# Routed token rows turned by a block exchange and VectorE instead of TensorE, with gathers eight tiles ahead and two raw weight buffers

## The chip, the cores and the metric

The kernel runs on one core of one Trainium2 chip. The metric is the device time of one execution in microseconds (us): the median of three runs. Times inside an execution come from the hardware profiler and count from the start of its span.

## The reference

The kernel computes one gated block: a state-space mixer whose result is added to x, and then a mixture of experts on the normalised sum. The part that the change touches is the second one.

```python
x = x + tanh(g_xattn) * mamba(ctx, layernorm(x))          # 4 x 512 tokens, width 512
h = layernorm(x).reshape(-1, 512)                         # 2048 tokens
scores = softmax(h @ gate_w.T)                            # 16 experts
topk_w, topk_ids = top_k(scores, 6); topk_w /= topk_w.sum(-1)
out = sum over experts e: combine[:, e] * swiglu(h, w13[e], w2[e])   # 6 of 16 per token
out = out + swiglu(h, sw13, sw2)                          # shared expert
x = x + tanh(g_ffn) * out
# swiglu(x, w13, w2): g, u = split(x @ w13.T); (silu(g) * u) @ w2.T, inner width 352 (704 shared)
```

## The kernel before

**Two stages.** For some 490 us the kernel runs the mixer, batch by batch (four batches, 16 states n, four channel blocks j per n). Orders of the side work per engine are written out by hand in tables (`PE_FIRST`, `SP_SECOND` and so on). In this stage GpSimd multiplies each scan by a row `crow` (L949), which SP loads three steps of n ahead (`c_row`, L576 to 582). When a batch's normalised rows are ready, SP stores them to a DRAM table `token_rows` (`rows`, L607), one DMA per batch, and later their 18 expert weights beside them (`weights`, L619).

**The experts** run in tiles of 128 tokens. The shared expert is cut into two of inner width 352, so there are 32 shared tiles (numbers 0 to 31, NS = 32), and then the routed tiles, each with tokens of one expert, 104 in this execution. A shared tile loads x already turned (channels on partitions) from a second table. A routed tile gathers 128 token rows by number with an indirect DMA on GpSimd (`gather`, L989) into one of four slots of `xt`, five tiles ahead (`AHEAD`), and TensorE turns it: four 128x128 transposes through an identity into PSUM bank 4 (`turn_x`, L1683). Each value is split into a high part rounded for TensorE and a low remainder, and each product is formed as high·high + high·low + low·high.

**One tile on TensorE** (`tile`, L1728), with the tile before it interleaved:

```python
up(t, s, (0, 1), off)                     # 12 products, N = 352
turn_a(t - 1, 1 - s)                      # 3 transposes, needs `am` of t-1
up(t, s, (2, 3), off)                     # 12 products
turn_x(t + 1, (s4 + 1) % 4, m)            # 4 transposes (routed tiles only)
down(t - 1, 1 - s, old)                   # 9 products, N = 512, needs `al` of t-1
```

Ahead of each routed tile TensorE's stream reads two registers from the table `meta` (`weights_of`, L1723: how many experts' weights must be there, L1724, and where they lie, L1726). Engines execute their streams in order.

**The other engines, per tile.** ScalarE: `ah` (high part of a, L862), `xh` (high part of x of the next tile, L852), silu (L857), copy of y (L868), then a register read that tells whether a new expert starts; if so it casts half of the next expert's weights (L822). VectorE: `al` (L1399), the tile's routing weight `cc` (L1372), the token numbers for the gather (`gather_ids`, L1378), `xl` (low part of x, L1363), the numbers for the output (L1383), the product `am` (L1393), and at an expert's start the other half of the cast (L1417). The copies L1372, L1378 and L1383 each follow a register read. GpSimd: gather, at an expert's start the low part of the weights (9.6 us, L987), and the accumulating indirect write of y to the output (`add`, L1011). The token numbers per expert are lists which GpSimd scatters to DRAM with 96 small DMAs beside the shared tiles and then reads back (L1060, `ids_in`).

**Weights.** One raw buffer `wraw`; SP fetches the next expert (2176 KB) as soon as the low part of the one before is done (`fetch`, L630), ScalarE's queue those of experts 1 and 2.

## Time and profile before

| | us |
|---|---|
| median of 3 runs | 1436.62 |
| lowest and highest run | 1435.21, 1438.37 |
| span of the profiled execution, core 0 | 1435.5 |
| mean granted TensorE clock | 0.976 |
| busy in the span: TensorE products / weight loads | 1349.9 / 1210.6 |
| busy: VectorE / ScalarE / GpSimd | 787.5 / 730.9 / 949.3 |

The profile gives the profiled execution's span and no other time of it; the runs' times are those of whole executions. A chain of waits, followed back from the last instruction, lies on TensorE for 65% of the span. "issue" in a row is time in which an engine waited for nothing that the profile shows. Products are pipelined: one begins while the one before still runs, so the rows' durations overlap, and the distance from start to start is what each costs. Some product records can be missing. Weight loads (PEld) and TensorE's products (PE) are shown as two engines, register reads of an engine's stream with a q behind the engine's name.

### The profile page before, as it was taken

To read this page: it belongs to the slowest core of one execution; us is meant where nothing else is said; L and a number is where in the kernel's file an instruction comes from. 1 tells how busy PE (TensorE), PEld (TensorE's weight loads), DVE (VectorE), ACT (ScalarE), POOL (GpSimd) and SP (SyncE) were. 2 spreads that over 40 slices of the span, in tenths; PEclk is the share of its full clock that TensorE was granted. 3 is DMA by queue.
4 is the path that set the end of the run, shared out by engine and by line. 5 is a ranking of instruction groups with operands and counts; after the bars stand their busy time and mean duration, and the time that the engine had idled before them with its cause. 6 is when DMAs were issued, how large, how long until landed. Compare 5 with 4: busy or idle time off the path is not lost.

```text
span 1435.5 us, 32257 instructions
## 1 busy us (share of the span) xinstructions
PE 1349.9 (94%) x8480; PEld 1210.6 (84%) x8481; DVE 787.5 (55%) x1364; ACT 730.9 (51%) x1317; POOL 949.3 (66%) x671
## 2 busy tenths in 40 slices
PE   6897998997898899999999999999999999999996
PEld 2686887887888799999998989989889988899885
DVE  6878898898989854653333333333333333333331
ACT  5898897898889464343332333323333333332321
POOL 0588898898988747887456665566645666546632
PEclk8899999999999999999999999999999999999999
DMA  4120122222242365645455435555445544454432
GB/s 137 38 74 31 53 67 96 67 73 91 75 146 72 133 129 106 142 84 141 83 141 145 131 63 144 139 147 137 104 94 137 141 135 104 95 147 131 76 68 36
DMA packets 65042, 149.13 MB, mean 104 GB/s; under 512 B 16976, under 2 KB 17616, under 8 KB 62656
## 3 DMA queue, kind: packets, MB, share of 16 engines
q0 software_dynamic: 31024, 62.10, 22.9%
q1 hardware_dynamic: 33392, 81.21, 17.5%
q10 hardware_dynamic: 560, 4.98, 1.0%
q8 instruction: 36, 0.59, 0.2%
q14 instruction: 30, 0.25, 0.1%
HBM read 101.50 MB, written 48.99 MB: 105 GB/s over the span
## 4 chain that ended last, share of the span: by engine, by line
PE 65%; DVE 3%; issue 1%; POOL 0%; ACT 0%; DVEq 0%; POOLq 0%; ACTq 0%
PE bank L1719 19%; PE bank L1699 19%; PE bank L1700 18%; PE bank L1687 3%; PE bank L1710 3%; DVE hs L1172 1%; PE bank L1604 1%; PE bank L1590 1%; PE bank L1602 0%; POOL hc L949 0%; DVE sc L1226 0%; PE bank L1665 0%; DVEq L1375 0%; DVE xl L1363 0%; DVE du L1186 0%
## 5 line engine op out<-in xcount | busy, mean ns | idle before, releaser
L949 POOL TENSOR_TENSOR hc<-hs,crow 128x512 f32<-128x512 f32 x254 | 322.6, 1302 | 91.8 <-DVE hs L1172 84.6
L1699 PE MATMUL bank<-w,xh 128*128 (+1 forms) x1088 | 368.7, 340 | 7.6 <-issue 4.2
L1015 POOL DMA_INDIRECT out_x<-ys,aid x104 | 171.2, 1646 | 275.0 <-issue 215.7
L1700 PE MATMUL bank<-w,xh 128*128 (+1 forms) x1088 | 351.2, 323 | 0.0
L1172 DVE TENSOR_TENSOR_SCAN hs<-dA,bank 128x512 f32<-128x512 f32 x256 | 295.8, 1208 | 47.9 <-PE bank L1604 32.0
L1719 PE MATMUL bank<-w,ah 128*128 (+1 forms) x816 | 264.7, 405 | 2.7 <-DVE al L1399 2.7
L1399 DVE TENSOR_TENSOR al<-bank,ah 128x384 fp32r<-128x384 f32 x136 | 75.8, 557 | 331.0 <-ACT ah L862 283.2
L1699 PEld LDWEIGHTS bank<-w,xh 128*128 128x128 f32 x1088 | 204.3, 188 | 35.9 <-issue 32.1
L1700 PEld LDWEIGHTS bank<-w,xh 128*128 128x128 f32 x1088 | 206.4, 190 | 2.3
L868 ACT COPY ys<-bank 128x512 f32<-128x512 f32 x136 | 79.9, 587 | 195.9 <-PE bank L1719 191.5
L1700 PE MATMUL bank<-w,xl 128*128 (+1 forms) x544 | 175.9, 323 | 0.0
L1699 PE MATMUL bank<-w,xl 128*128 (+1 forms) x544 | 175.7, 323 | 0.0
L1719 PEld LDWEIGHTS bank<-w,ah 128*128 128x128 f32 x816 | 145.0, 189 | 27.7 <-issue 2.2
L1590 PE MATMUL bank<-ident,hc 128*128 128x128 f32 x1024 | 160.4, 281 | 7.6 <-POOL hc L949 5.1
L862 ACT CAST ah<-bank 128x384 fp32r<-128x384 f32 x136 | 65.3, 480 | 196.9 <-PE bank L1710 166.7
L786 ACT ACTIVATE dA<-delta,aneg 128x512 f32<-128x512 f32 x256 | 164.0, 710 | 0.0
L1604 PE MATMUL bank<-bdiag,duT 128*128 128x128 f32 x1024 | 163.7, 285 | 0.0
L1719 PE MATMUL bank<-w,al 128*128 (+1 forms) x408 | 161.2, 395 | 0.0
L852 ACT CAST xh<-bank 128x512 fp32r<-128x512 f32 x104 | 61.2, 588 | 182.9 <-PE bank L1687 175.4
L987 POOL TENSOR_TENSOR w<-wraw,w 128x4352 f32 x15 | 143.8, 9588 | 0.7 <-issue 0.5
L1604 PEld LDWEIGHTS bank<-bdiag,duT 128*128 128x128 f32 x1024 | 142.5, 201 | 0.0
L1590 PEld LDWEIGHTS bank<-ident,hc 128*128 128x128 f32 x1024 | 124.3, 145 | 11.0 <-POOL hc L949 6.7
(184 smaller groups left out, 2051.7 us busy)
## 6 DMA issues: line engine op xcount, KB each, us to landing
wraw<-in_wall SPq DMA_DIRECT2D x16, 2176.0 KB
crow<-c_rows SPq DMA_DIRECT2D x64, 256.0 KB, 3.3
xt<-token_rows_turned SPq DMA_DIRECT2D x32, 256.0 KB
out_x<-ys POOLq DMA_DIRECT2D x32, 256.0 KB
wraw<-in_wall ACTq DMA_DIRECT2D x2, 2176.0 KB
token_rows<-rowb SPq DMA_DIRECT2D x4, 1028.0 KB
xrow<-in_x SPq DMA_DIRECT2D x4, 1024.0 KB, 7.0
out_x<-xrow SPq DMA_DIRECT2D x4, 1024.0 KB, 4.9
```

Of the source, the lines that this page charges most:

```text
L786: nc.scalar.activation(dA[:, 4 * (n % 2) + j, :], delta[b % 2][:, j, :], ACT.Exp, scale=aneg[:, j, n:n + 1]).then_inc(dA_done, 1)
L868: nc.scalar.copy(ys[:, slot, :], banks[7][:]).then_inc(ys_done, 1)
L949: nc.gpsimd.tensor_tensor(hc[:, j, :], hs[:, j, :], crow[:, n % 4, :], ALU.mult).then_inc(hc_done, 1)
L987: nc.gpsimd.tensor_tensor(columns(w, at + WCOLS, WCOLS), wraw[:], columns(w, at, WCOLS), ALU.subtract).then_inc(wl_done, 1)
L1015: pool.indirect_dma_start(out_rows, bass.IndirectOffsetOnAxis(ap=aid[:, s:s + 1], axis=0), ys[:, s, :], None, bounds_check=TOKENS - 1, oob ...
L1172: nc.vector.tensor_tensor_scan(hs[:, j, :], dA[:, 4 * (n % 2) + j, :], dbu[j % 2][:], 0.0, ALU.mult, ALU.add).then_inc(scanned, 1)
L1399: nc.vector.tensor_tensor(al[:, s, :], banks[5][:, 0:IP], ah[:, s, :], ALU.subtract).then_inc(al_done, 1)
L1590: mm = nc.tensor.matmul(ysum[t][:, cols], hc[:, j, t * P:(t + 1) * P], ident[:], start=n == 0 and j == 0, stop=n == DS - 1, is_transpose=T ...
L1604: mm = nc.tensor.matmul(dbu[j % 2][:, t * P:(t + 1) * P], duT[b % 2][:, t, j * P:(j + 1) * P], bdiag[:, n % 2, t - COPIED, :], start=True, ...
L1699: nc.tensor.matmul(gate_bank[:, 0:I], xx, columns(w, off + ww + k * 2 * I, I), start=first, stop=last)
L1700: mm = nc.tensor.matmul(up_bank[:, 0:I], xx, columns(w, off + ww + k * 2 * I + I, I), start=first, stop=last)
L1719: mm = nc.tensor.matmul(banks[7][:], aa, columns(w, off + ww + W2AT + k * H, H), start=k == 0 and n == 0, stop=k == IK - 1 and n == 2)
```

## The change

TensorE no longer turns x of routed tiles. Rows are stored to `token_rows` with their 512 values regrouped by 32-wide quadrants: 16 DMAs per batch and one for two more columns, in place of one. The gather goes into a new buffer `rowg`, eight tiles ahead in place of five. For each pair of tiles SP exchanges blocks between quadrants of partitions with 16 DMAs of 32 partitions x 2 tiles x 512 B from `rowg` to `xq` (which lies in `wraw`, free after the shared experts). VectorE then transposes 32x32 blocks of `xq` into PSUM bank 4 (`turn`), ahead of `al`. The routing weight is taken three tiles ahead, the token numbers seven; the first of these move to earlier shared tiles, and with them VectorE's wait for the lists. Weights of experts from 2 on are fetched on ScalarE's queue into two raw buffers `wnext`; ScalarE reads one more register per tile for it.

```diff
-AHEAD = 5
-FIRST_ROWS = {NS - 3: (NS, NS + 1), NS - 2: (NS + 2,), NS - 1: (NS + 3, NS + 4)}
+AHEAD = 8
+TAKEN = 3
+FIRST_IDS = {NS - 4: (NS, NS + 1, NS + 2, NS + 3), NS - 2: (NS + 4, NS + 5), NS - 1: (NS + 6,)}
+FIRST_TAKEN = {NS - 1: (NS, NS + 1, NS + 2)}
+FIRST_ROWS = {NS - 5: (NS, NS + 1), NS - 4: (NS + 2, NS + 3), NS - 2: (NS + 4, NS + 5), NS - 1: (NS + 6, NS + 7)}
...
+        xq = wraw[:, 0:4 * H].rearrange("p (s c) -> p s c", s=4)
...
+        rowg = alloc(ctx, "rowg", [P, 4, ROW])
+        wnext = alloc(ctx, "wnext", [P, 2 * WCOLS])
...
             def rows(b, _):
                 sp.wait_ge(norm_done, TC * (b + 1))
-                sp.dma_start(rows_v[b, :, :, 0:H + 2], rowb[:]).then_inc(rows_stored, 16)
+                    for t in range(TC):
+                        for c in range(QUAD):
+                            sp.dma_start(rows_v[b, :, t, c * P:(c + 1) * P].rearrange("p (k i) -> p k i", k=HK),
+                                         rowb[:, t, 0:H].rearrange("p (k c i) -> p c k i", k=HK, c=QUAD)[:, c]).then_inc(rows_stored, 16)
+                    sp.dma_start(rows_v[b, :, :, H:H + 2], rowb[:, :, H:H + 2]).then_inc(rows_stored, 16)
...
-            with sp.Fori(3, NX) as e:
-                fetch(e)
+            def exchange(i, h):
+                for k in (2 * h, 2 * h + 1):
+                    apart(sp, gathered[k], 16 * i + 16, "sp")
+                apart(sp, xt_turned, 4 * i + NS + 2 * h - 2, "sp")
+                for q in range(QUAD):
+                    for c in range(QUAD):
+                        sp.dma_start(xq[32 * c:32 * c + 32, 2 * h:2 * h + 2, q * P:(q + 1) * P],
+                                     rowg[32 * q:32 * q + 32, 2 * h:2 * h + 2, c * P:(c + 1) * P]).then_inc(swapped[h], 16)
...
+            with sp.Fori(0, groups) as i:
+                for h in range(2):
+                    exchange(i, h)
...
             def next_weights(t):
...
                     split_high(e, t)
+                last = act.value_load(meta[0:1, 5, bass.ds(t, 1)], min_val=0, max_val=NX - 2)
+                with act.If(last > 0):
+                    apart(act, wl_done, last, "act")
+                    fetch(last + 1)
...
-            def gather(t, s):
-                if isinstance(t, int) and t < NS + 4:
-                    pool.wait_ge(xl_done, t - 3)
-                else:
-                    apart(pool, xt_turned, t - 3, "pool")
+            def gather(t, s, m):
+                if not (isinstance(m, int) and m == 0):
+                    apart(pool, swapped[s // 2], 16 * QUAD * QUAD * m, "pool")
                     apart(pool, cc_done, t - 3, "pool")
                 apart(pool, gid_done, t + 1, "pool")
-                pool.indirect_dma_start(xt[:, s, :], None, rows_d[:, :],
+                pool.indirect_dma_start(rowg[:, s, :], None, rows_d[:, :],
...
+            def turn(t, s4, m):
+                if isinstance(t, int) and t < NS:
+                    return
+                apart(dve, swapped[s4 // 2], 16 * QUAD * QUAD * (m + 1), "dve")
+                dve.wait_ge(xh_done, t)
+                dve.wait_ge(xl_done, t)
+                nc.vector.transpose(banks[4][:].rearrange("p (k q j) -> p q k j", k=HK, q=QUAD),
+                                    xq[:, s4, :].rearrange("p (q k i) -> p q k i", q=QUAD, k=HK)).then_inc(xt_turned, 1)
...
-            def gather_ids(t, s4):
+            def gather_ids(t, s4, m):
+                if not (isinstance(m, int) and m == 0):
+                    apart(dve, gathered[s4], 16 * m, "dve")
...
-            def tile(t, s4, gathers=False, adds=False, m=None):
+            def tile(t, s4, m=0, gathers=False, takes=False, adds=False):
                 s = s4 % 2
+                turn(t + 1, (s4 + 1) % 4, m + (s4 + 1) // 4)
                 a_low(t - 1, 1 - s)
-                take_weight(t + 1, (s4 + 1) % 4, m)
...
+                    for late in FIRST_IDS.get(t, ()):
+                        gather_ids(late, late % 4, (late - NS) // 4)
+                    for late in FIRST_TAKEN.get(t, ()):
+                        take_weight(late, late % 4, (late - NS) // 4)
+                if takes:
+                    take_weight(t + TAKEN, (s4 + TAKEN) % 4, m + (s4 + TAKEN) // 4)
+                if gathers:
+                    gather_ids(t + AHEAD - 1, (s4 + AHEAD - 1) % 4, m + (s4 + AHEAD - 1) // 4)
                 x_low(t + 1, 1 - s)
...
-                if t == NS - 3:
+                if t == min(FIRST_IDS):
                     dve.wait_ge(ids_in, 16)
...
-                if more and not (isinstance(t, int) and t + 1 < NS):
-                    turn_x(t + 1, (s4 + 1) % 4, m)
                 down(t - 1, 1 - s, old() if callable(old) else old)
```

## Rows read from the trace of the kernel before

**Rows 1.** The page: busy time of an engine, and one of its costliest groups

```profile
PE 1349.9 (94%) x8480; PEld 1210.6 (84%) x8481; DVE 787.5 (55%) x1364; ACT 730.9 (51%) x1317; POOL 949.3 (66%) x671
...
L949 POOL TENSOR_TENSOR hc<-hs,crow 128x512 f32<-128x512 f32 x254 | 322.6, 1302 | 91.8 <-DVE hs L1172 84.6
```

**Rows 2.** Busy time by stretch (stretch, length, engines, granted clock, DMA share, GB/s)

```profile
1000.00:1200.00 200.00, 197.80 (x1154) 179.75 (x1153) 71.59 (x179) 66.45 (x120) 113.20 (x62) 1.00 0.48 118
```

**Rows 3.** Timeline (start, us, engine, line): `a` transposes of shared and routed tiles

```profile
675.36 0.49 PE L1710 MATMUL bank<-ident,am 128*128 128x128 f32 x3
681.65 0.49 PE L1710 MATMUL bank<-ident,am 128*128 128x128 f32 x3
694.68 0.49 PE L1710 MATMUL bank<-ident,am 128*128 128x128 f32 x3
...
1407.53 0.49 PE L1710 MATMUL bank<-ident,am 128*128 128x128 f32 x3
```

**Rows 4.** Timeline of TensorE in one routed tile; in brackets the idle time before

```profile
1005.50 0.49 PE L1710 MATMUL bank<-ident,am 128*128 128x128 f32 x3
...
1007.76 0.60 PE L1687 MATMUL bank<-ident,xt 128*128 128x128 f32 x4
1008.12 0.71 PE L1719 MATMUL bank<-w,ah 128*128 x2
...
1010.06 0.40 PE L1719 MATMUL bank<-w,al 128*128 x1
...
1010.48 0.19 PEld L1699 LDWEIGHTS bank<-w,xh 128*128 128x128 f32 x1 [0.45 <-issue]
```

**Rows 5.** Timeline of ScalarE and VectorE in the same tile

```profile
1006.02 0.48 ACT L862 CAST ah<-bank 128x384 fp32r<-128x384 f32 x1 [1.46 <-PE bank L1710]
...
1006.54 0.56 DVE L1399 TENSOR_TENSOR al<-bank,ah 128x384 fp32r<-128x384 f32 x1 [2.24 <-ACT ah L862]
...
1009.02 0.69 DVE L1363 TENSOR_TENSOR xl<-bank,xh 128x512 fp32r<-128x512 f32 x1 [0.35 <-ACT xh L852]
```

**Rows 6.** Line L1724, ns min/median/max, first and last start: that tile; 780 to 1435

```profile
L1724 PEldq TENSOR_LOAD <-meta x1: 897/897/897, 1008.0 to 1008.0; - x1
...
L1724 PEldq TENSOR_LOAD <-meta x92: 296/452/1000, 780.2 to 1411.3; - x92
```

**Rows 7.** Timeline of GpSimd, the accumulating write before that load

```profile
1005.61 1.59 POOL L1015 DMA_INDIRECT out_x<-ys,aid  x1 [4.11 <-issue]
```

**Rows 8.** Timeline of a tile in which an expert starts

```profile
845.99 2.02 ACT L822 CAST w<-wraw 128x2176 f32 x1 [0.50 <-issue]
...
850.91 0.69 DVE L1363 TENSOR_TENSOR xl<-bank,xh 128x512 fp32r<-128x512 f32 x1
...
851.86 0.43 PE L1699 MATMUL bank<-w,xh 128*128 x1 [0.24 <-DVE xl L1363]
```

**Rows 9.** The lists' load and its landing (us), and VectorE around it

```profile
678.11 0.59 POOL L1060 DMA_DIRECT2D lists<-token_lists  x1 [0.47 <-DMA token_lists<-ids,posi]
...
DMA to landing us min/median/max: 3.8/3.8/3.8
...
676.40 0.56 DVE L1399 TENSOR_TENSOR al<-bank,ah 128x384 fp32r<-128x384 f32 x1 [3.79 <-issue]
...
682.69 0.56 DVE L1399 TENSOR_TENSOR al<-bank,ah 128x384 fp32r<-128x384 f32 x1 [3.79 <-ACT ah L862]
683.83 0.15 DVE L1378 COPY gid<-lists 128x1 int32 x1 [0.58 <-issue]
```

**Rows 10.** Line L582, SP's `crow` loads: ns of an issue, and landing (us)

```profile
L582 SPq DMA_DIRECT2D crow<-c_rows x64: 319/320/1097, 23.3 to 468.1; - x64
...
DMA to landing us min/median/max: 3.0/3.3/7.8
```

**Rows 11.** Busy time by stretch around an idle spell (columns as in rows 2)

```profile
228.00:230.00 2.00, 0.37 (x4) 0.13 (x2) 1.97 (x4) 2.00 (x4) 1.57 (x3) 1.00 0.56 130
...
232.00:234.00 2.00, 2.00 (x12) 2.00 (x12) 1.28 (x2) 0.00 (x0) 1.74 (x3) 0.53 0.00 0
```

More of the change, by code:

```diff
@@ L447, in mamba_moe @@
         gathered = [sem(f"gathered{i}") for i in range(4)]
+        swapped = [sem(f"swapped{i}") for i in range(2)]
+        cc_done = sem("cc_done")
         zero_done = sem("zero_done")
@@ L608, in rows @@
                 sp.wait_ge(norm_done, TC * (b + 1))
-                sp.dma_start(rows_v[b, :, :, 0:H + 2], rowb[:]).then_inc(rows_stored, 16)
+                with nc.allow_non_contiguous_dma(reason="a row's columns by quadrant of the transposed row"):
+                    for t in range(TC):
[3 more added lines that the diff above has]
+                    sp.dma_start(rows_v[b, :, :, H:H + 2], rowb[:, :, H:H + 2]).then_inc(rows_stored, 16)
             def turned_(b, _):
@@ L886, in high_piece @@
                     act.wait_ge(down_done, TT * (e - 1))
-                nc.scalar.copy(w[:, base + at:base + at + size], wraw[:, at:at + size]).then_inc(*split(e, k, EARLY))
+                raw, first = raw_of(e)
+                nc.scalar.copy(w[:, base + at:base + at + size], raw[:, first + at:first + at + size]).then_inc(*split(e, k, EARLY))
             def last_choice(_):
@@ L1071, in _ @@
             for k in range(8):
-                if k + AHEAD < 8:
-                    gather(rest + k + AHEAD, (k + AHEAD) % 4)
                 next_weights(rest + k)
@@ L1485, in _ @@
                     dve.sem_inc(aid_done, NS)
-                tile(t, t % 4)
+                tile(t, t % 4, -1 if t < NS else 0)
                 beside(DVE_AFTER_MUL, t)
@@ L1489, in _ @@
             groups = routed_groups(dve)
-            tile(PEELED, PEELED % 4)
+            tile(PEELED, PEELED % 4, -1)
             next_weights(PEELED)
-            for k in range(1, 4):
-                tile(PEELED + k, (PEELED + k) % 4, True, True)
-                next_weights(PEELED + k)
-            with dve.Fori(0, groups - 1) as i:
+            for t in range(NS, NS + 3):
+                tile(t, t % 4, 0, gathers=True, takes=True, adds=True)
+                next_weights(t)
+            most = groups_but_2(dve)
+            with dve.Fori(0, most) as i:
                 for k in range(4):
                     t = 4 * i + NS + 3 + k
-                    tile(t, (3 + k) % 4, True, True, i + 1)
+                    tile(t, (3 + k) % 4, i + (3 + k) // 4, gathers=True, takes=True, adds=True)
                     next_weights(t)
-            last = tiles_but_12(dve) + 11
-            a_low(last - 1, 0)
-            add_ids(last, 3)
-            multiply(last, 1)
-            a_low(last, 1)
+            rest = tiles_but_12(dve) + 7
+            for k in range(4):
+                tile(rest + k, (3 + k) % 4, most + (3 + k) // 4, takes=k < 2, adds=True)
+                next_weights(rest + k)
+            a_low(rest + 3, 0)
+            add_ids(rest + 4, 3)
+            multiply(rest + 4, 3, most + 1)
+            a_low(rest + 4, 1)
         @block.tensor
@@ L1681, in beside @@
                         last_count(i)
-            def turn_x(t, s, m=None):
-                rows_in(pe, t, s, m, "pe")
-                at_least(pe, xl_done, t)
-                for k in range(HK):
-                    mm = nc.tensor.transpose(banks[4][:, k * P:(k + 1) * P], xt[:, s, k * P:(k + 1) * P], ident[:])
-                mm.then_inc(xt_turned, 1)
             def up(t, s, chunks, off):
@@ L1726, in weights_of, with tile @@
                 return pe.value_load(meta[0:1, 1, bass.ds(t, 1)], min_val=0, max_val=2 * WCOLS)
-            def tile(t, s4, old, off, more=True, m=None):
+            def tile(t, s4, old, off):
                 s = s4 % 2
@@ L1764, in _ @@
                     off = weights_of(4 * i + PEELED + k)
-                    tile(4 * i + PEELED + k, (3 + k) % 4, old, off, True, i)
+                    tile(4 * i + PEELED + k, (3 + k) % 4, old, off)
                     old = off
@@ L1770, in of_last @@
                 return pe.value_load(meta[0:1, 1, bass.ds(last - k, 1)], min_val=0, max_val=2 * WCOLS)
-            tile(last, 3, lambda: of_last(1), weights_of(last), False)
+            tile(last, 3, lambda: of_last(1), weights_of(last))
             turn_a(last, 1)
```

83 lines of the change are left out of this document (49 added, 34 removed).

## Prediction

> **What bounds the kernel now.** I read the page first, then the stretches, then single tiles. The page shows TensorE busy for 94% of the span [rows 1], the windows 98.9% of it (197.80 of 200 us) in the routed stage [rows 2]. That looks like an engine limited by its products, from which every removed microsecond comes off the end. The single tiles say something else. A shared tile, which turns no x, takes 681.65 − 675.36 = 6.29 us from one set of three `a` transposes to the next; from 694.68 to 1407.53 there are 103 periods of 6.92 us [rows 3]. The four x transposes hold the array for 1008.12 − 1007.76 = 0.36 us, and I take 0.35 [rows 4]. They explain a bit over half of the 0.63 us between the two kinds of tile.
>
> The rest is TensorE's instruction stream. In the tile whose `a` transposes start at 1005.50 (T), ScalarE rounds `a` from T+0.52, VectorE has the low half (`al`) at 1006.54 + 0.56 = T+1.60 [rows 5], and only then does the stream pass its wait, hand out `down`, and start two register loads for the next tile (`weights_of`, L1724 and L1726). The first begins at 1008.0 and takes 897 ns [rows 6]; the next tile's first weight load comes at 1010.48 = T+4.98, after 0.45 us of idling that nothing else explains ("issue") [rows 4]. The array could have begun at T+4.80: the last `down` product starts at 1010.06, and the nine are some 0.24 us apart. So there are **two limits on the start of the next tile**: the array, T+4.80, and the stream, which is 0.9 us (hand-out) + the first load + 1.58 us (1010.48 − 1008.90) behind `al`: T+4.38 with the shortest load (296 ns), T+4.98 with this one. The median load in the routed stage is 452 ns, the longest 1000 [rows 6]. The stream's limit starts at `al`, which comes before the x transposes, so removing them doesn't move it.
>
> Why loads are long: GpSimd's accumulating write of the tile before started at 1005.61, the load ended at 1008.90, 3.3 us later [rows 6, 7]. A load that begins while that write is under way ends about there.
>
> **The change part by part, against the profiled execution** (span 1435.5 us; the median of the runs shown is 1436.6, and I set the sum against that, as 1.1 us lies outside the span or is scatter).
>
> *x transposes off TensorE.* Array limit T+4.45 in place of T+4.80. Were it the only limit: 104 × 0.35 = 36 us. The stream gives part of it back. The accumulating write waits for the tile's y, and y for the end of `down`, so with `down` 0.35 us earlier the write comes earlier too. Let u be the start of a tile's successor after T: a late u puts the next T later, the write relatively earlier, its load shorter, and the next u earlier by as much. Two successive u thus add up to a constant, now about 4.80 + 4.98, afterwards 0.35 less. Each tile gains half: 0.175 us, and 104 × 0.175 = **−18.2 us**. At an expert's start the chain is another but the same holds: ScalarE's cast of weights (845.99, 2.02 us) holds back `al`, then `xl` (850.91) and the next tile to 851.86 [rows 8]; that cast follows the y of the tile before, which moves with `down`.
>
> *VectorE's turn.* The trace has no such operation. Nearest row: `xl`, 128x512 out of PSUM, 0.69 us [rows 5]; I bound it by that and twice that, 1.38, and take 0.7. It stands ahead of `al`, where VectorE sits 2.24 us until ScalarE is done [rows 5], so it costs nothing; without that cover it would be 104 × 0.7. At an expert's start the idle is shorter, and 1.38 us would cost 0.3 in 15 tiles. The Trainium skill (VectorE: DVE Perf Modes, Rules for kernel authors) says to transpose 128×128 on TensorE when PSUM will do, and gives 311 ns on VectorE for 128 columns of bf16: an estimate of 4 × 311 = 1.24 us for 512 columns, by which the sum stays as it is.
>
> *Other VectorE work.* `gather_ids` gains a wait in front of `xl`. `xl` itself needs no TensorE turn any more, but in part of the tiles it is the id copy ahead of it that decides. Two register steps, some 0.1 us: +2.4 us (0 to 5).
>
> *The start of the routed stage.* The wait for the token lists moves one tile ahead. The lists are issued at 678.11 and land 3.8 us later, at 681.9; the id copies of today come at 683.83 and just don't wait. One tile earlier VectorE stands at the `al` of 676.40 [rows 9], so it stops for 5.5 us, and TensorE with it. `down` then starts at 682.6 instead of 677.6. Four id copies follow in front of `xl`: the first 1.14 us after `al` starts (683.83 − 682.69), three more of some 0.73 (0.58 idle + 0.15), then 0.15 and `xl`, 0.69, and 0.26 to the first product (851.86 behind 850.91 + 0.69 [rows 8]): 686.4 instead of 675.36 + 4.45 = 679.8. **+6.6 us.** GpSimd sends the lists behind its own scatters of token numbers, so nothing in this change brings them sooner. In tile 31 one id and three weights stand ahead of `xl` (5.47 against 4.80): +0.7. After an idle stretch as long as this the clock may fall: at 228 to 230 the engine worked 0.37 of 2 us, and at 232 to 234 it was granted 0.53, the lower level of 1.2 GHz [rows 11]. Three microseconds at half speed lose 1.5, partly inside the wait: +1.0 (0 to 3).
>
> *The exchange.* 16 DMAs of 32 KB for two tiles on SP. An issue on SP takes 0.32 us at the median [rows 10]: 5.1 us per pair, landing some 3.3 later, against 2 × 6.7 us. With gathers eight tiles ahead a pair has about 1.5 tiles to spare. It costs nothing on the path. But it reads SBUF all through the stage, as the accumulating write does that stretches the loads: per load between nothing and the 0.6 us of 897 against 296; it can't shorten them. Pieces of 32 KB, spread out, are a thinner stream than one write of 256 KB, so I stay near the lower end: 0.02 each, **+2 us** (0 to 28; the upper end is 0.2 us, worked out under the rivals).
>
> *Weights.* The fetches move from SP to ScalarE's queue, one issue per expert behind the cast, and each tile reads one register more: about 0.6 us, within the 1.46 us that ScalarE idles before `ah` [rows 5]. On SP they would have stood ahead of the exchange. GpSimd's gather waits for later ids, still long before its write is due: nothing.
>
> *Rows stored in 16 + 1 pieces.* 17 SP issues in place of one, 5.4 us, with `crow` loads behind them. These are asked for three steps of n ahead, each four products of 1.30 us on GpSimd [rows 1]: 15.6 us, and land in 3.3, 7.8 at worst [rows 10]. 5.4 + 7.8 < 15.6: nothing (0 to 3).
>
> Sum: −18.2 + 2.4 + 6.6 + 0.7 + 1.0 + 2.0 = −5.5, so **1431.1 us**, and I say 1431. The forecast's own range is 1422 to 1440.
>
> **The rivals.**
> *The array is the only limit* (0.17). For it: 98.9% busy [rows 2]. Then −36.4 + 8.3 (list wait, tile 31, clock) = 1408. Against it: the 0.45 us "issue" ahead of the weight load [rows 4].
> *Slower, by longer register loads* (0.25). If the exchange's reads stretch the first load of each tile by 0.2 us, the stream's limit takes the gain: with every tile 0.2 later and the array no longer deciding, the steady tiles lose about 104 × 0.18 = 19 us in place of gaining 16, and the start loses 8.3: 1464. At 0.1 us gain and loss are even in the tiles and the start's loss remains: 1445. The point from which it decides is 0.05 us per load. For it: loads of 897 against 296 beside another SBUF-reading DMA; against it: gathers and weight fetches go on beside loads now, and the shortest still take 296.
> *The exchange doesn't keep pace* (0.04). Two `crow` issues took up to 1.10 us [rows 10]; 16 × 1.10 = 17.6 us per pair would bind the stage: 52 × (17.6 − 13.5) = +213, 1650. Here the Trainium skill (DMA: Bandwidth & Descriptors, Rules for kernel authors) warns that many small transfers should be coalesced and that under 64 KB it is mostly overhead. By that rule this rival would get more; the row's median of 0.32 speaks against it.
> *Nothing to see* (0.09): the steady gain comes to about 9 us and the start's loss eats it, 1436.
>
> **How the numbers follow.** About 0.2% (2.9 us) is what a measurement of this kernel can tell from no change. The forecast holds 0.45; by its own range about 0.07 of it lies within 0.2% and 0.02 above. Faster: 0.17 + 0.36 = 0.53. Same: 0.07 + 0.09 = 0.16. Slower: 0.25 + 0.04 + 0.02 = 0.31. For 8 in 10 the range reaches from the array's case, 1408, to 1450, which leaves out the worse half of the slower case and the lost pace.
>
> **What would show it.** Right: tile periods near 6.75 in the routed stage with weight loads idle on "issue"; a gap of about 5 us on TensorE at 677 to 683; `al` still 1.6 us behind the `a` transposes. Wrong: periods of 6.4 (the array alone), first loads above 0.5 us at the median (the stretch), TensorE or VectorE waiting for `xq` (the pace), or no gap at the start.

## The result and the profile after

The changed kernel takes 1491.52 us (median of 4 runs, 1488.31 to 1493.88) beside 1437.49 us for the kernel before on the same chip: a ratio of 1.0374 with an interval of 1.0354 to 1.0394. It is 54 us slower, where 6 us less were forecast. The profiled span went from 1435.5 to 1492.0 us, the mean granted clock from 0.976 to 0.955.

TensorE has 11 us less work (1338.9 against 1349.9 us [rows 1]) and is idle longer. These are the page's line of busy times and the windows row that answers to [rows 2]:

```profile
PE 1338.9 (90%) x8064; PEld 1184.5 (79%) x8065; DVE 857.2 (57%) x1469; ACT 732.2 (49%) x1317; POOL 949.1 (64%) x671
...
1000.00:1200.00 200.00, 181.36 (x966) 161.25 (x965) 83.37 (x189) 62.30 (x111) 107.59 (x56) 0.96 0.62 148
```

In the same 200 us TensorE worked 181.36 us, before 197.80. Where it stood idle is told by its waits in the routed stage (700 to 1440; columns: us in total, times, longest):

```profile
PE bank L1772 <- DVE am L1452: 42.2, 10, 5.3
PE bank L1761 <- issue: 14.2, 42, 1.0
PE bank L1761 <- DVE xl L1410: 4.2, 7, 1.1
PE bank L1781 <- DVE al L1458: 3.5, 10, 0.8
```

The first line is new: ten waits ahead of the `a` transposes (`turn_a`, now L1772) for VectorE's `am`, up to 5.3 us each. I write T for the start of a tile's three `a` transposes, as in the prediction. Here is the timeline around one such wait. Tile 58, in which an expert starts, has T = 914.91:

```profile
914.91 0.49 PE L1772 MATMUL bank<-ident,am 128*128 128x128 f32 x3
...
929.69 0.99 POOL L1041 DMA_INDIRECT rowg<-token_rows,gid  x1 [9.46 <-issue]
930.85 9.59 POOL L1033 TENSOR_TENSOR w<-wnext,w  x1 [0.18 <-issue]
...
934.88 0.49 PE L1772 MATMUL bank<-ident,am 128*128 128x128 f32 x3
940.61 1.59 POOL L1059 DMA_INDIRECT out_x<-ys,aid  x1 [0.17 <-issue]
...
946.25 0.15 DVE L1441 COPY aid<-lists 128x1 int32 x1 [7.62 <-DMA out_x<-ys,aid]
946.51 0.58 DVE L1452 SCALAR_TENSOR_TENSOR am<-sg,cc,bank 128x352 f32<-128x352 f32 x1
...
947.15 0.90 PE L1772 MATMUL bank<-ident,am 128*128 128x128 f32 x3 [5.32 <-DVE am L1452]
```

Read it upwards. TensorE waits for `am`, `am` stands behind the id copy `aid` on VectorE, `aid` waits 7.62 us for the landing of the accumulating write of four tiles earlier (four slots), and that write was issued at 940.61, T+25.7. Its y had been copied by 920.46 (T+5.6); it stood behind the 9.6 us low part of the weights (`split_low`), and that behind the gather, which GpSimd issued only at T+14.8 after 9.46 us of waiting. In the kernel before, the same three instructions at an expert's start are these, with the start of that tile, 52, and the `aid` of four tiles later:

```profile
846.66 0.49 PE L1710 MATMUL bank<-ident,am 128*128 128x128 f32 x3
...
848.91 0.98 POOL L997 DMA_INDIRECT xt<-token_rows,gid  x1 [0.30 <-issue]
849.91 9.58 POOL L987 TENSOR_TENSOR w<-wraw,w 128x4352 f32 x1
859.65 1.58 POOL L1015 DMA_INDIRECT out_x<-ys,aid  x1 [0.16 <-issue]
...
871.95 0.15 DVE L1383 COPY aid<-lists 128x1 int32 x1 [0.36 <-issue]
```

Gather at T+2.2, write at T+13.0, `aid` at T+25.3. No `aid` waited for a write there; after the change ten do (who waited for the write's line L1059 from 700 to 1430, and its landing):

```profile
  DVE aid L1441: 64.0, 10
...
DMA to landing us min/median/max: 4.6/5.4/11.5
```

What did the gather wait for? It writes a slot of `rowg` that the exchange of four tiles earlier reads. This is the exchange's line, first for the 16 DMAs of that pair, then for the whole run (ns of an issue, min/median/max), with who waited for it in the whole run:

```profile
L688 SPq DMA_DIRECT2D wraw<-rowg x16: 594/602/1103, 910.8 to 921.0; - x16
...
  POOL rowg L1041: 9.5, 1
...
L688 SPq DMA_DIRECT2D wraw<-rowg x832: 588/597/1517, 692.8 to 1446.4; - x167
...
  POOL rowg L1041: 178.9, 25
  DVE bank L1426: 12.6, 9
```

An issue takes 0.60 us, so a pair takes 11.3 us here (910.8 to 922.1), and after the last issue the gather still waits until 929.69, while the next expert's weights pass: ScalarE asked for them at 915.07, and the DMA engines are full from 915 to 925 (windows, the last but one column is their share):

```profile
915.00:920.00 5.00, 4.71 (x26) 3.79 (x24) 2.57 (x7) 2.50 (x5) 3.94 (x3) 1.00 0.95 323
920.00:925.00 5.00, 5.00 (x31) 4.85 (x32) 2.07 (x5) 1.89 (x4) 0.23 (x1) 1.00 1.02 303
```

The pairs that the gathers of the nine stalled starts wait for land 6.5 to 9.1 us after their last issue has ended, the other 43 pairs 1.3 us after it at the median and 4.7 at the most.

All fifteen expert starts fit. Two tiles share one exchange, so only the gather in an even tile, the first of its pair, meets this wait. In the nine starts in even tiles (32, 38, 52, 58, 64, 70, 84, 90, 116) the gather goes at T+13.8 to T+15.3 and the write at T+24.6 to T+26.1, and the third and fourth period after the start (T of tile t+3 to T of tile t+5 for a start in tile t) are together 3.6 to 7.1 us longer than the same two before: 53.6 us. In the six in odd tiles (45, 77, 97, 103, 109, 123) the write goes at T+16.1 to T+20.8, and these two periods differ by −0.4 to +0.9 us. Part of each stall is the clock after it: in all nine the granted clock fell to 0.50, for 3.4 to 6.9 us. In tile 61 TensorE works 0.83 of 6 us, and then runs at half speed, the level of 1.2 GHz, for 3 us (windows; the granted clock is the third column from the right):

```profile
941.00:947.00 6.00, 0.83 (x6) 0.53 (x4) 0.65 (x2) 0.00 (x0) 4.78 (x5) 0.76 0.66 111
947.00:950.00 3.00, 2.85 (x11) 2.86 (x12) 1.41 (x4) 1.06 (x2) 2.56 (x2) 0.50 0.89 175
```

The second loss is at the start. VectorE's `al` stops as forecast, but longer:

```profile
674.04 0.35 ACTq L880 DMA_DIRECT2D wnext<-in_wall  x1
...
682.84 0.59 POOL L1104 DMA_DIRECT2D lists<-token_lists  x1 [4.85 <-DMA token_lists<-ids,posi]
685.57 0.56 DVE L1458 TENSOR_TENSOR al<-bank,ah 128x384 fp32r<-128x384 f32 x1 [12.61 <-DMA lists<-token_lists]
...
688.92 0.71 DVE L1410 TENSOR_TENSOR xl<-xt,xh 128x512 fp32r<-128x512 f32 x1
```

The lists are issued at 682.84 instead of 678.11 [rows 9], since GpSimd waits 4.85 us for its scatters to land, before 0.5.

**The account**, from T to T: tiles 26 to 30 are 10.6 us longer, 30 to 32 0.6, the nine stalls 53.6, the other 84 tiles up to 134 are 9.8 us shorter, the shared tiles before 0.2 longer: 55.2 of the 56.5 us by which the spans differ; the rest lies before the first and after the last tile.

### The profile page after: what moved, and what is told of

Same layout as the page of the kernel before. It is cut to its first block, busy times and chain, and to the rows that moved or that the text cites. A ratio compares the mean times of both kernels' runs of the same rounds, so it can differ in the third digit from the quotient of the medians.

```text
span 1492.0 us, 33495 instructions
## 1 busy us (share of the span) xinstructions
PE 1338.9 (90%) x8064; PEld 1184.5 (79%) x8065; DVE 857.2 (57%) x1469; ACT 732.2 (49%) x1317; POOL 949.1 (64%) x671
## 3 DMA queue, kind: packets, MB, share of 16 engines
q0 software_dynamic: 31024, 62.10, 22.6%
## 4 chain that ended last, share of the span: by engine, by line
PE 27%; DMA 10%; SPq 9%; issue 9%; POOL 7%; DVE 4%; POOLq 2%; DVEq 2%; ACTq 1%; ACT 1%
SPq L688 9%; PE bank L1781 8%; PE bank L1761 7%; PE bank L1762 7%; POOL token_lists L1071 5%; DMA rowg<-token_rows,gid 5%; DMA wraw<-rowg 2%; DMA out_x<-ys,aid 2%; PE bank L1772 2%; POOL out_x L1053 1%; DVE hs L1214 1%; DVEq L1430 1%; POOLq L1076 1%; POOLq L1082 1%; PE bank L1673 1%
## 5 line engine op out<-in xcount | busy, mean ns | idle before, releaser
L1761 PE MATMUL bank<-w,xh 128*128 (+1 forms) x1088 | 379.1, 349 | 20.4 <-issue 15.3
L1762 PE MATMUL bank<-w,xh 128*128 (+1 forms) x1088 | 357.0, 329 | 0.0
L1781 PE MATMUL bank<-w,ah 128*128 (+1 forms) x816 | 261.0, 401 | 15.1 <-DVE al L1458 15.0
L1041 POOL DMA_INDIRECT rowg<-token_rows,gid x104 | 105.0, 1010 | 265.3 <-issue 195.1
L1761 PEld LDWEIGHTS bank<-w,xh 128*128 128x128 f32 x1088 | 209.6, 193 | 60.6 <-issue 57.7
L1059 POOL DMA_INDIRECT out_x<-ys,aid x104 | 168.3, 1618 | 102.4 <-ACT ys L908 45.1
L1762 PEld LDWEIGHTS bank<-w,xh 128*128 128x128 f32 x1088 | 211.3, 194 | 1.4
L1781 PEld LDWEIGHTS bank<-w,ah 128*128 128x128 f32 x816 | 152.3, 192 | 43.5 <-issue 10.3
L1762 PE MATMUL bank<-w,xl 128*128 (+1 forms) x544 | 178.5, 328 | 0.0
L1761 PE MATMUL bank<-w,xl 128*128 (+1 forms) x544 | 178.4, 328 | 0.0
L1033 POOL TENSOR_TENSOR w<-wnext,w x15 | 144.0, 9600 | 0.8 <-issue 0.2
```

The source lines that it names most:

```text
L1033: nc.gpsimd.tensor_tensor(columns(w, at + WCOLS, WCOLS), columns(raw, source, WCOLS), columns(w, at, WCOLS), ALU.subtract).then_inc(wl_don ...
L1041: pool.indirect_dma_start(rowg[:, s, :], None, rows_d[:, :], bass.IndirectOffsetOnAxis(ap=gid[:, s:s + 1], axis=0)).then_inc(gathered[s], 16)
L1059: pool.indirect_dma_start(out_rows, bass.IndirectOffsetOnAxis(ap=aid[:, s:s + 1], axis=0), ys[:, s, :], None, bounds_check=TOKENS - 1, oob ...
L1761: nc.tensor.matmul(gate_bank[:, 0:I], xx, columns(w, off + ww + k * 2 * I, I), start=first, stop=last)
L1762: mm = nc.tensor.matmul(up_bank[:, 0:I], xx, columns(w, off + ww + k * 2 * I + I, I), start=first, stop=last)
L1781: mm = nc.tensor.matmul(banks[7][:], aa, columns(w, off + ww + W2AT + k * H, H), start=k == 0 and n == 0, stop=k == IK - 1 and n == 2)
```

## The experiments

The table holds the two stretches of each profiled execution, T26 to T32 (start) and T32 to T134 (102 routed periods); executions differ by up to 4.6 us before tile 26 (T26 lies between 664.96 and 669.55), which these leave out. Ratios are against the kernel before, on the same chip; e2, e3 and e4 are single runs, and only their times stand. e2 and e5 leave a part of the routed x out of the computation.

| run | time, us | ratio (interval) | T26 to T32 | T32 to T134 |
|---|---|---|---|---|
| before | 1437.5 | 1 | 39.1 | 707.0 |
| after | 1491.5 | 1.0374 (1.0354 to 1.0394) | 50.4 | 750.9 |
| e1 gather last | 1441.1 | 1.0026 (1.0011 to 1.0042) | 49.5 | 702.0 |
| e2 half the exchange | 1439.2 | | 50.1 | 697.7 |
| e3 fetch two tiles later | 1449.0 | | 49.9 | 706.1 |
| e4 third fetch in tile 22 | 1485.8 | | 46.3 | 748.3 |
| e5 before, one x transpose | 1423.5 | 0.9909 (0.9889 to 0.9930) | 38.7 | 693.2 |
| e6 e1 + start | 1439.6 | 1.0017 (1.0005 to 1.0029) | 46.4 | 699.1 |
| e7 e6, write held | 1441.3 | 1.0030 (1.0016 to 1.0045) | 47.1 | 700.9 |
| e8 before, write held | 1478.9 | 1.0302 (1.0281 to 1.0323) | 39.1 | 748.4 |
| e9 before, loads ahead of `down` | 1443.3 | 1.0028 (1.0013 to 1.0044) | 39.7 | 712.3 |
| e10 e6, loads ahead of `down` | 1432.9 | 0.9965 (0.9952 to 0.9978) | 46.3 | 693.5 |
| e11 e10, scatters earlier | 1433.4 | 0.9963 (0.9950 to 0.9976) | 46.7 | 695.9 |
| e12 before, loads ahead of `turn_a` | 1487.6 | 1.0339 (1.0321 to 1.0357) | 41.8 | 752.7 |
| e13 after, all edits, loads as e12 | 1477.4 | 1.0278 (1.0260 to 1.0296) | 43.4 | 740.7 |
| e14 before, loads ahead in two of four | 1431.9 | 0.9961 (0.9946 to 0.9975) | 39.3 | 701.0 |
| e15 after, all edits, loads as e14 | 1426.6 | 0.9911 (0.9892 to 0.9930) | 40.9 | 692.0 |

**What makes the write late (e1, e2, e3).** Three things stand one behind the other: the exchange's 16 issues, the weight fetch beside its landing, and the order on GpSimd. Each run takes away one.

```diff
 e1, GpSimd's routed loop
-                    gather(t + AHEAD, (k + AHEAD) % 4, i + (k + AHEAD) // 4)
                     next_weights(t)
                     expert_starts(t, k)
                     add(t, k)
+                    gather(t + AHEAD, (k + AHEAD) % 4, i + (k + AHEAD) // 4)
 e2, exchange (and its two counts halved)
-                    for c in range(QUAD):
+                    for c in range(0, QUAD, 2):
 e3, ScalarE's next_weights
-                last = act.value_load(meta[0:1, 5, bass.ds(t, 1)], ...
+                last = act.value_load(meta[0:1, 5, bass.ds(t - 2, 1)], ...
```

> The changed kernel with one edit: in GpSimd's routed loop the gather stands behind the accumulating write of the tile in place of ahead of everything. Theory A (GpSimd's order): at an expert's start in an even tile the gather waits for an exchange until 13.8 to 15.3 us after the tile's a transposes (T), the 9.6 us split_low and the tile's write are queued behind it (write at T+25), and VectorE waits four tiles later for that write. With the gather last, split_low starts at about T+4 and the write at about T+14, as in the kernel before; the nine stalls of 3.6 to 7.1 us (53.6 us in sum) go: 1491.5 - 53.6 = 1438, between 1430 and 1448, and no wait of VectorE's id copy (aid) on the write is left above 1 us. Rival B (the exchange's own pace: 16 issues of 0.60 us for two tiles, landing up to 6.9 us late): the gathers now go no earlier than before, at expert starts later, so the exchange comes later still and VectorE's turn waits for it: 1480 to 1510.

> The changed kernel with 8 in place of 16 exchange DMAs for two tiles: half of the 32x32-block columns of each routed x are not moved (left out of the computation). Theory A, as to where the time is lost: the exchange of a pair ends 8 x 0.62 = 5 us earlier, an even expert start's gather goes at about T+9 to T+10, its write at about T+20, where the six starts in odd tiles have it today without a stall: the nine stalls go or fall under 1 us each, 1438 to 1446. Rival C (the weight fetch on ScalarE's queue is what makes the exchange late, by 5.6 to 6.9 us between last issue and landing): the shorter exchange overlaps the fetch as much and lands as late: stalls shrink by less than half, 1465 to 1485.

> The changed kernel with ScalarE asking for the weights of the expert after next two tiles after an expert's start in place of at the start. Rival C (the fetch beside the exchange makes it land late): the exchange that an even expert start's gather waits for lands about 5 us earlier, the write goes at about T+20, and the nine stalls go: 1438 to 1446; the odd starts may get stalls of their own if the fetch now meets their exchange. Theory A with the issue cost alone deciding: the gather's time moves by less than 2 us and the stalls stay at 4 to 6 us each: 1475 to 1490.

e1 came out at 1441, within Theory A's range. At the start in tile 58 (T = 894.50) GpSimd now does this:

```profile
894.50 0.49 PE L1772 MATMUL bank<-ident,am 128*128 128x128 f32 x3
896.98 1.00 POOL L1041 DMA_INDIRECT rowg<-token_rows,gid  x1 [0.30 <-issue]
898.00 9.62 POOL L1033 TENSOR_TENSOR w<-wnext,w  x1
...
907.78 1.58 POOL L1059 DMA_INDIRECT out_x<-ys,aid  x1 [0.17 <-issue]
```

The gather there is the tile before's; `split_low` starts at T+3.5 and the write at T+13.3, as in the kernel before. No wait of `aid` for a write is left, nor any of `turn_a` for `am`; the nine stalls come to 0.9 us in place of 53.6, and T32 to T134 falls by 48.8 us. The exchange keeps up: VectorE's turn waits for it 12.1 us in seven tiles. Rival B falls.

e2 (1439) and e3 (1449) take away nearly as much, 53.1 and 44.8 us, with GpSimd's order left as it was. So no single part is the cause. In the changed kernel the writes at the fifteen starts land 4.5 to 5.1 us after their issue, and one that went by about T+20 held TensorE up by 0.6 us at the most (in e3, with writes at T+16.0 to T+22.6, by 1.7); to pass that it took the long exchange, the fetch beside it and the 9.6 us behind the wait together. Rival C's expectation for e2 fell and Theory A's for e3 fell, by the same fault: each took one part to be enough by itself. What the three runs share is the place, the wait in front of `split_low` and the write.

**The same stall in the kernel before (e8).** Here the exchange and its issues don't exist; the write alone is held back, by 5.5 us at the median of the tiles in and just behind which no expert starts (T+12.3 in place of T+6.8). Meant as a test of the register loads (below), it shows the stall.

```diff
                     expert_starts(t, k)
+                    apart(pool, xl_done, t + 4, "pool")
                     add(t, k)
```

> The kernel before, its x transposes kept, with the same hold of GpSimd's accumulating write behind VectorE's xl. Theory L: tiles whose first register load is short take 6.74 us there, those with the write at the a transposes 7.00 (66 of 102); all at 6.74 is (6.93 - 6.74) x 102 = 19 us less, 1418, between 1414 and 1424, with the median first load 0.30 in place of 0.41 us. Rival (the array alone is the limit, loads don't matter): 1434 to 1440.

It came out 3% slower. These are the start in tile 58 (T = 893.17) with the landing of its write, TensorE's waits from 700 to 1440, and who waited for the write from 700 to 1430:

```profile
901.14 0.98 POOL L997 DMA_INDIRECT xt<-token_rows,gid  x1 [0.31 <-issue]
902.15 9.59 POOL L987 TENSOR_TENSOR w<-wraw,w 128x4352 f32 x1
...
911.90 0.33 SPq L633 DMA_DIRECT2D wraw<-in_wall  x1
911.91 1.59 POOL L1015 DMA_INDIRECT out_x<-ys,aid  x1 [0.17 <-issue]
...
DMA to landing us min/median/max: 10.4/10.4/10.4
...
PE bank L1711 <- DVE am L1394: 35.0, 13, 4.4
...
  DVE aid L1384: 60.4, 13
```

The held write of the tile before pushes the gather to T+8.0 and `split_low` to T+9.0; the write comes at T+18.7 in place of T+13, and thirteen tiles wait for `am`. A kernel without any exchange stalls in the same place once GpSimd is some 6 us late at an expert's start. I had priced that lateness at nothing. What counts is when the write has landed: in this kernel SP fetches the next weights in the moment in which the write goes (911.90), and the writes at fourteen of the fifteen starts land 9.2 to 10.4 us after their issue, so that T+18.7 is too late here and would not be in the changed kernel.

The third and fourth periods after the fifteen starts are together 44.5 us longer than in the kernel before. The rest of the 102 periods gain 3.2 us, although the first register load of a tile now takes 0.303 us at the median (700 to 1400) in place of 0.385. The 19 us that Theory L gave to short loads did not come.

**The start (e4, e6, e11).**

```diff
 e4
-               8: [("exp", 3)], TT - 3: [("fetch", 2)], NS - 5: [("fetch", 3)]}
+               8: [("exp", 3)], TT - 3: [("fetch", 2)], NS - 10: [("fetch", 3)]}
 e6: e1, e4 and
-FIRST_IDS = {NS - 4: ...
+FIRST_IDS = {NS - 3: ...
-FIRST_ROWS = {NS - 5: (NS, NS + 1), NS - 4: (NS + 2, NS + 3), ...
+FIRST_ROWS = {NS - 4: (NS, NS + 1), NS - 3: (NS + 2, NS + 3), ...
 e11: e10 and
-LISTS_LATE = 2
+LISTS_LATE = 1
```

> The changed kernel with the fetch of the third expert's weights (2.2 MB, ScalarE's queue) in tile 22 in place of tile 27. Theory S (the start's extra loss): this fetch, at 674.0, runs beside the last scatters of token numbers, which land 4.3 us later than before (GpSimd waits 4.85 in place of 0.5 us for them), so the lists go out at 682.8 in place of 678.1 and the first routed tiles come that much later. With the fetch done before, GpSimd waits under 1 us, the lists go out at about 678, the gap between the a transposes of tiles 26 and 27 is 12.3 in place of 17.0 us and the whole 4.7 us less: 1487. Rival: the scatters land late for another reason (rows stored in pieces, the small descriptors): nothing changes, 1491.

> The changed kernel with three edits: the gather last in GpSimd's routed loop (as alone in e1), the fetch of the third expert's weights in tile 22 (as alone in e4), and the first token ids and gathers one tile later, where the kernel before waits for the lists. If the terms add: 1441 (e1) - 4.7 (lists sooner) - 1 (part of the wait for the lists hidden again; the chain lists, gather, 16 exchange issues, turn is some 19 us long and binds the first routed tile in either place): 1435, between 1431 and 1439, level with the kernel before.

> e10 with GpSimd's scatters of token numbers one tile earlier throughout (they begin one tile after the shared stage's first tile in place of two, and end 3 to 6 us earlier), so that the lists land before VectorE asks for them and the chain lists, gather, exchange, turn begins sooner: 4 to 6 us less than e10. Rival (the first exchange is bound by SP's issues whatever the lists do, or GpSimd's writes are late now): no change against e10.

e4's lists and the `al` that waits for them:

```profile
675.87 0.59 POOL L1104 DMA_DIRECT2D lists<-token_lists  x1 [0.45 <-DMA token_lists<-ids,posi]
679.75 0.56 DVE L1458 TENSOR_TENSOR al<-bank,ah 128x384 fp32r<-128x384 f32 x1 [9.33 <-DMA lists<-token_lists]
```

GpSimd waits 0.45 us again; tiles 26 to 30 take 32.1 us in place of 36.3, against 25.6 before. So with the lists on time the wait that the change moved ahead costs 6.5 us, against the 6.6 for the wait and 1.0 for the clock of the prediction, and the fetch beside the scatters the other 4.2. e6, with 1439.6 just above its range, gains nothing at the start by asking later: 46.4 as in e4, the loss only passes to tiles 30 to 32, where the turn waits up to 9.1 us for the first exchange. e11 sends the lists a tile sooner and gains nothing either, with the tile in which they are asked for as late as in e10. Lists sooner and asked for in the changed kernel's tile (e13, e15) do it: 43.4 and 40.9 us.

**What the x transposes are worth (e5).**

```diff
-                for k in range(HK):
+                for k in range(1):
                     mm = nc.tensor.transpose(banks[4][:, k * P:(k + 1) * P], xt[:, s, k * P:(k + 1) * P], ident[:])
```

> The kernel before with one in place of four x transposes per routed tile: three quarters of the routed x are left out of the computation (xl and xh are taken from a bank of which three quarters are not written anew). It measures the term x transposes off TensorE by itself, 3/4 of it. The prediction's half share (two limits, array and instruction stream, in turn): 104 x 0.75 x 0.35 / 2 = 13.7 us less: 1423, between 1419 and 1427. Rival (the array is the only limit): 104 x 0.75 x 0.35 = 27.3 us less: 1409, between 1405 and 1413. Rival (the instruction stream alone decides): within 3 us of 1437.

1423.5 us, and T32 to T134 13.9 us shorter where the half share said 13.7. The half share holds; scaled to four transposes it is 18.5 us, the prediction 18.2. What halves the gain, e5 doesn't show by itself.

**The stream's register loads (e7, e9, e10, e12 to e15).** Once the stalls are gone the routed tiles take 6.85 to 6.88 us (e6, e1), and by my estimate the array would allow 6.40 (6.74 for the shortest kinds of tile of the kernel before, less 0.35). Theory L says that TensorE's register loads hold them.

```diff
 e7: e6, with the write held as in e8 and the gather between split_low and it
 e9 (before), e10 (e6): loads for the next tile, k < 3 of four
                 up(t, s, (2, 3), off)
+                coming = ahead() if ahead else None
...
                 down(t - 1, 1 - s, old() if callable(old) else old)
 e12 (before), e13: the same line and old()'s load, ahead of turn_a(t - 1, 1 - s)
 e14 (before), e15: as e9, in k = 1 and 2 alone
 e13 and e15 also have e1, e4 and LISTS_LATE = 1
```

> As e6, but GpSimd's accumulating write waits besides for VectorE's xl of the tile after next (3 us after the a transposes of the next tile in place of 0.3 before them), with the gather between split_low and it. Theory L (the two limits): the steady tiles still lose because a register load of TensorE that begins while the write reads SBUF is long (0.58 to 0.77 us in tiles of 7.0 to 7.2 us, 0.30 in tiles of 6.4 to 6.6); with the write moved behind the loads the array alone sets the tile, 6.40 in place of 6.88 us mean: 102 x 0.4 = 41 less of which expert starts keep some: 1400 to 1415. Rival: the write moved there delays VectorE's id loads or the next waits by as much, or the exchange does the stretching by itself: 1428 to 1440.

> The kernel before, x transposes kept, with the two register loads for the next tile placed on TensorE's stream ahead of down's wait for al in place of behind down, in three of every four tiles (the fourth is the loop's seam). Theory L (two limits): the stream no longer decides in these tiles, they take the array's 6.74 us in place of 6.93: 102 x 0.75 x 0.19 = 14.5 us less, 1423, between 1417 and 1429. Rival (the held writes of e8 helped nothing because loads do not matter): 1435 to 1440.

> e6 (gather last, the start's two edits) with the same early register loads. Theory L: without x transposes the array allows 6.40 us and the stream with two loads of 0.30 us allows just the same 6.40, so that every longer load and the loop's seam show; with the loads early three in four tiles go to 6.40 from a mean of 6.85: 102 x 0.75 x 0.45 = 34 us less than e6's 1440, less what VectorE's xl and am, a few tenths behind, still hold back (10): 1416, between 1405 and 1425. Rival (the exchange, 70% of the DMA engines' time, or VectorE holds the tile at 6.8): 1432 to 1441.

> The kernel before, x transposes kept, with the register loads for the next tile, and the reload of the last tile's offset at the loop's seam, ahead of turn_a's wait for am (which ends 1.4 us before the array is ready for turn_a) in place of behind or ahead of down. Theory L: in e9 two tiles of four reached the array's 6.74, the one with three loads ahead of down took 7.2 to 7.4, the seam 6.95; with the loads at turn_a three tiles of four at 6.74 and the seam at 6.95 give 6.79 in place of 6.93: 102 x 0.14 = 14 us less, 1423, between 1418 and 1430. Rival (the loads hold turn_a in turn, or the array starves there): 1436 to 1445.

> The changed kernel with the gather last in GpSimd's loop, the third expert's weights fetched in tile 22, the scatters of token numbers one tile earlier with the first ids and gathers where the changed kernel has them, and the register loads ahead of turn_a as in e12. Against e10 (1433): the lists land before tile 28 asks for them, the first exchange begins one tile earlier and the turn of tile 32 no longer waits 9 us for it: 6 us less; the tile with three loads ahead of down goes from 7.0 to 6.5: 25 x 0.5 = 12 us less: 1415, between 1408 and 1425. Rival (VectorE and the exchange hold the tiles at 6.8, the start is bound by SP's issues): 1428 to 1434.

> The kernel before, x transposes kept, with the two register loads for the next tile ahead of down's wait in two tiles of four (the two that reached 6.74 us in e9), behind down as before in the other two. Theory L: these two kinds of tile go from means of 6.81 and 6.88 to 6.74, the others stay: 25 x (0.07 + 0.14) = 5 us less, 1432.5, between 1429 and 1436. Rival (a tile that ends sooner only meets the write of the tile before later in the next one, and the sum stays): 1436 to 1441.

> The changed kernel with the gather last in GpSimd's loop, the third expert's weights fetched in tile 22, the scatters of token numbers one tile earlier with the first ids and gathers where the changed kernel has them, and the early register loads in two tiles of four as in e14. Against e10 (1433): e13's start, 43.4 us from tile 26 to 32 in place of 46.3, 3 less; the tile with three loads ahead of down from 7.01 to about 6.84, 4 less: 1426, between 1421 and 1432. Rival (as in e14, the tiles give each other back what they gain): 1430 to 1437.

e7 missed: 700.9 us against e6's 699.1. e9 missed as a whole, but by position in the loop of four it is plain: two of the four kinds of tile fall from means of 6.81 and 6.87 to 6.74 and 6.73 (without the tiles in which an expert starts), which I take for the array's time, and the one with a third load ahead of `down` rises from 6.78 to 7.35. e10 gains 5.6 us on e6 in T32 to T134 where 24 were expected; its time lies in the range of its rival, by which the exchange or VectorE holds the tile at 6.8. e12 was worst; two rows, of TensorE's weight loads and of its products, show why:

```profile
903.60 0.31 PEld L1710 LDWEIGHTS bank<-ident,am 128*128 128x128 f32 x3 [1.51 <-issue]
...
903.63 0.52 PE L1710 MATMUL bank<-ident,am 128*128 128x128 f32 x3 [1.25 <-issue]
```

Three loads ahead of `turn_a` used up the lead of the stream: no weights were loaded for 1.51 us, and the array stood empty for 1.25. e13, with the same loads, loses for the same reason. e14 puts the loads only where e9 gained, and e15 is the changed kernel with every edit that the runs support: 1431.9 and 1426.6 us where 1432.5 and 1426 were expected. **e15 beats both kernels**: the kernel before on the same chip by 0.9%, and the changed kernel, which ran on another, by 4.4%. Not all of the 0.9% is the change's: against e14, the kernel before with its loads in the same two kinds of tile, e15 is 5.4 us faster (1426.6 against 1431.9).

## Why the prediction was wrong

**The step that failed** reads: "GpSimd's gather waits for later ids, still long before its write is due: nothing." I looked at the ids, not at the other wait that the diff gives the gather, the exchange of four tiles earlier, and did not name what stands behind it: at an expert's start 9.6 us of `split_low` and then the write. In its place the runs showed 53.6 us in nine of fifteen starts, taken away by e1 without touching anything else, and made anew by e8 in the kernel before.

**The price that hid it** is in the exchange: "An issue on SP takes 0.32 us at the median [rows 10]: 5.1 us per pair ... With gathers eight tiles ahead a pair has about 1.5 tiles to spare. It costs nothing on the path." An issue takes 0.597 us at the median, a pair 10.2 to 11.7, and beside a weight fetch the gather behind it went 7.6 us after the last issue. The `crow` loads move 128 partitions x 2048 B, the exchange 32 partitions x 2 x 512 B; I took the price of one for the other. (Whether the shape makes the difference, or that the exchange stays within SBUF, no run separates.) VectorE had to wait for the exchange itself for only 12.6 us, in nine tiles, so the rival "doesn't keep pace" was wrong in its mechanism too; the loop through GpSimd was not among my cases. In the prediction I set aside the rule of the Trainium skill (DMA: Bandwidth & Descriptors, Rules for kernel authors) that small transfers pay mostly overhead; here the trace sides with the rule: 16 transfers of 32 KB held SP for at least 10.2 us.

**The start.** The terms 6.6 for the wait and 1.0 for the clock came to 6.5 together (e4). Missing were 4.2 us: I wrote that "nothing in this change brings them sooner", but a line of the change that stands in e4's edit, the fetch of the third expert's weights in tile 27, sends the lists out later.

**Right, by their own steps.** The x transposes: −18.2 forecast, −18.5 by e5, so half of the transposes' time and not all of it. VectorE's turn: taken as 0.7 us and hidden, measured 0.725 (L1426), with TensorE waiting 3.5 us for `al` in all; the estimate of 1.24 us from the figure of the Trainium skill (VectorE: DVE Perf Modes, The three transpose paths) was too high for this case. Rows in 17 pieces: the first `a` transposes come 0.2 us later, which is within the scatter of the executions, though the issue of a piece took 0.53 us at the median (L631) and not 0.32. Weights on ScalarE's queue: its issue is hidden as said, its transfer is not.

**Mis-sized or not met.** Longer register loads, the rival with a quarter of the chance, did not happen. From 700 to 1400 the first load's median fell (before, then after):

```profile
L1724 PEldq TENSOR_LOAD <-meta x101: 296/385/1000, 703.9 to 1396.3; - x101
...
L1786 PEldq TENSOR_LOAD <-meta x95: 297/307/977, 701.8 to 1398.9; - x95
```

The writes had moved away from the loads: before, a write started within 0.25 us of T in 66 of 102 routed tiles, after in 10. The prediction's reading that a load begun under a write ends about with it holds in one stretch alone: in the kernel before, 47 of the 49 first loads begun 2.2 to 2.9 us after a write's start ended 3.3 to 3.4 us after it, while the 16 begun 0.3 to 1.9 us after it took 0.30 us. The steady tiles gained 9.8 us in 84 tiles, 0.12 each, where −18.2 + 2.4 + 2.0 said 0.13 (no run measures the 2.4 and the 2.0 by themselves). That is partly luck of the late writes: in e1 and e6, without the stalls and with a write beside T in 20 and 18 tiles, the same 84 tiles gain 5.9 and 7.3 us, and the whole stage 5.0 and 7.9, not 13.8. Of the missing 6 to 9 us, e14 shows that the order of the register loads can give back 6.1 in the kernel before. By my estimate the array's limit without x transposes, 6.40 us, lies level with what the stream allows with two short loads, so that every longer load, the loop's seam and a late `xl` would show. In e15, from 700 to 1395, TensorE's products wait 12.6 us for VectorE's `xl`, `am` and `al`, and 14.8 us on "issue". How the remaining 0.4 us per tile divides stays open.

## What to carry over

A wait that a change adds to an in-order engine is priced by what is queued behind it, in the worst tile and not in the usual one: here a 9.6 us instruction that comes in one tile of seven. Look for the buffer whose free slot closes the loop (four slots of `aid` and `ys`), and work out how late its write may land before someone waits, with the landing in that very tile. `aid` comes at T+25.3. At an expert's start the changed kernel's write lands 5 us after its issue, which leaves T+20 for a write that used to go at T+13; a gather that waits for 16 DMA issues and a fetch uses up these seven microseconds. In the kernel before the same write lands 9 to 10 us after its issue, beside a fetch, and has two or three. A DMA issue is priced by rows of the same shape between the same places, and a transfer moved to a quiet queue still meets the others on the DMA engines.

## What the runs showed of the hardware

- SP's issue of a DMA of 32 partitions x 2 x 512 B between SBUF places takes 588 ns at the least, 597 at the median; that of 128 partitions x 2048 B took 320 [rows 10]. Halving the number of issues left the price as it was (e2: 588/597/1477).
- An accumulating write lands 5.4 us after its issue at the median, up to 11.5. One that goes together with the fetch of an expert's weights (e8) takes 9.2 to 10.4. While the weights of an expert passed (915 to 925), the gather that waited for the exchange went 7.6 us after the last of its issues had ended (922.1 to 929.69).
- A register load on TensorE's stream costs far more than its own 0.30 us where the stream has no lead: three of them ahead of `turn_a` emptied the array for 1.25 us (e12), while two ahead of `down` were free in two kinds of tile. A first load that begins 2.2 to 2.9 us after the start of an accumulating write ends 3.3 to 3.4 us after that start (47 of 49 in the kernel before), so it takes up to 1.0 us.
- VectorE turns 128x512 f32 in blocks of 32x32 from SBUF to PSUM in 725 ns on average (104 of them).
